# Opening of a fused gated cross-attention kernel: spare buffers for the second batch's turned tiles, another order of the first copies, identity products ahead of the first projections

## The reference, cut to what matters

```python
x = x + tanh(g_xattn[0]) * xattn(layernorm(x), ctx, pos, pos, Wq, Wkv, Wout, bout)
x = x + tanh(g_ffn[0]) * ffn(layernorm(x), up_w, down_w, expert_weight, ln_gamma, ln_beta)

# xattn: 16 batches, 256 rows, 512 columns, 32 heads of 16, context of 256 columns
q = rope(x @ Wq); k, v = split(ctx @ Wkv); k = rope(k)
attn = softmax(q @ k.T / 4) @ v
return attn @ Wout + bout
```

## Time and profile before

| what | us |
| --- | --- |
| median of the runs | 1657.44 |
| lowest and highest of the runs (3) | 1647.83 and 1659.67 |
| the profiled execution | 1645.12 |
| its span, from the first to the last instruction | 1643.3 |
| mean granted clock of TensorE in it | 0.982 |

### The profile page before, as it was taken

One profiled execution on the slowest core, in us unless ns is written; L12 is line 12 of the kernel. 1 busy time (PEld: TensorE's weight loads), 2 busy tenths in 40 slices (PEclk: granted clock), 3 DMA queues, 4 the chain that ended last, 5 costly groups with the idle time before them and its releaser, 6 DMA issues.

```text
span 1643.3 us, 27815 instructions
## 1 busy us (share of the span) xinstructions
PE 1558.6 (95%) x9760; PEld 1159.0 (71%) x9760; DVE 974.3 (59%) x1448; ACT 639.1 (39%) x962; POOL 295.5 (18%) x370
## 2 busy tenths in 40 slices
PE   6499999999999999988799999999999999999998
PEld 4356666666666666654578787887878878788786
DVE  6578887788777778865464543535435354263524
ACT  3155555555555555556342222222222222222221
POOL 5222222222222222201000210102101021020202
PEclk9699999999999999999899999999999999999999
DMA  4714444444444444333340110101101011010101
GB/s 141 158 47 112 121 108 117 123 123 116 116 104 103 106 102 116 96 94 99 115 135 20 45 33 10 48 20 46 32 1 53 25 46 32 1 51 26 36 16 39
DMA packets 67138, 120.53 MB, mean 73 GB/s; under 512 B 12280, under 2 KB 25720, under 8 KB 67064
## 3 DMA queue, kind: packets, MB, share of 16 engines
q1 hardware_dynamic: 67064, 119.50, 27.4%
HBM read 51.17 MB, written 16.78 MB: 41 GB/s over the span
## 4 chain that ended last, share of the span: by engine, by line
PE 82%; DVE 10%; issue 4%; ACT 1%; SPq 1%; POOL 1%; DMA 1%; DVEq 0%; POOLq 0%; ACTq 0%
PE pP L959 16%; PE pA L1142 11%; PE pO L959 11%; PE pB L1142 10%; PE pT L959 10%; PE pA L1044 6%; PE pO L1068 6%; PE pM L959 4%; DVE mneg L1339 3%; PE pB L1056 2%; PE pT L966 2%; PE pP L966 2%; PE pM L966 2%; PE pM L1109 1%; SPq L493 1%
## 5 line engine op out<-in xcount | busy, mean ns | idle before, releaser
L1339 DVE TENSOR_REDUCE mneg<-pA 128x4 f32<-128x1024 f32 x250 | 305.5, 1222 | 142.5 <-PE pA L1044 140.7
L864 ACT ACTIVATE probs<-pB 128x1024 f32<-128x1024 f32 x256 | 262.4, 1025 | 262.5 <-PE pB L1056 257.3
L1439 DVE TENSOR_TENSOR relu<-relu 128x512 f32<-128x512 f32 x128 | 88.2, 689 | 261.3 <-ACT hid L917 261.2
L687 POOL TENSOR_SCALAR var_eps<-meanvar 128x1 f32<-128x1 f32 x96 | 34.6, 360 | 1074.3 <-DVE meanvar L1231 1074.3
L1142 PE MATMUL pA<-dn,hid 128*128 128x512 f32 x768 | 199.0, 394 | 1.6 <-DVE hid L1441 0.9
L1142 PE MATMUL pB<-dn,hid 128*128 128x512 f32 x768 | 196.0, 390 | 0.0
L959 PE MATMUL pP<-fT,up 128*128 128x512 f32 x768 | 190.0, 396 | 0.0
L959 PE MATMUL pO<-fT,up 128*128 128x512 f32 x768 | 187.3, 393 | 0.0
L1142 PEld LDWEIGHTS pA<-dn,hid 128*128 128x128 f32 x768 | 142.9, 188 | 37.2 <-DVE hid L1441 5.9
L959 PEld LDWEIGHTS pO<-fT,up 128*128 128x128 f32 x768 | 144.5, 188 | 32.3 <-issue 0.4
L1142 PEld LDWEIGHTS pB<-dn,hid 128*128 128x128 f32 x768 | 144.2, 188 | 31.0
(11 more groups left out here) (177 smaller groups left out, 1958.1 us busy)
## 6 DMA issues: line engine op xcount, KB each, us to landing
stk<-kT SPq DMA_DIRECT2D x192, 128.0 KB, 2.9
stq<-qT SPq DMA_DIRECT2D x192, 128.0 KB, 3.0
xin<-x SPq DMA_DIRECT2D x32, 256.0 KB, 2.8
xres<-x SPq DMA_DIRECT2D x32, 256.0 KB, 3.0
x_scratch<-xres SPq DMA_DIRECT2D x32, 256.0 KB, 2.0
fx<-x_scratch SPq DMA_DIRECT2D x32, 256.0 KB, 2.7
fres<-x_scratch SPq DMA_DIRECT2D x32, 256.0 KB, 2.8
out<-y_s SPq DMA_DIRECT2D x32, 256.0 KB, 2.0
```

What stands on the lines that cost most here:

```text
L687: nc.gpsimd.tensor_scalar_add(var_eps[:], meanvar[:, 1:2], EPS).then_inc(ve_made, 1)
L864: nc.scalar.activation(probs[:, s % 4, :, :, :].rearrange("p a b s -> p a (b s)"), pB[:, :, :], ACT.Exp).then_inc(exp_done, 1)
L1339: nc.vector.tensor_reduce(mneg[par][:, :, 2 * u:2 * u + 2].rearrange("p t q -> p q t"), psum[:, :, :].rearrange("p q (t k) -> p q t k", t= ...
L1439: nc.vector.tensor_tensor(r[:], r[:], r[:], ALU.mult).then_inc(sq_made, 1)
```

## The change

- The turned tiles of batch 1 go to buffers that are idle in the opening: `k1T` (hi and lo) in parts 1 and 2 of `probs`, `q1T` in `av_s` (`turned_tiles`). So ACT no longer waits for the stack copies of batch 0 there. The copies of batch 1 count on semaphores of their own (`second_in`). ACT's first exponential, which writes `probs`, waits instead for all of batch 1's copies (`stack_in`).
- `rot2` has two buffers, taken in turn, and DVE's wait on POOL is one sum looser.
- SP issues the copies of the first half of the heads (k, then q) ahead of those of the second half, for both batches.
- ACT rounds all four query weight chunks ahead of the tables, and POOL splits chunks 2 and 3 ahead of `inv_std(2)`.
- `keep_awake` puts 22 products of the identity with itself ahead of X0 of batch 0, 28 ahead of K0 and 8 ahead of Q0, into a PSUM bank that the opening uses only later.

The diff:

```diff
--- before.py
+++ after.py
@@ -101,6 +101,7 @@
     ("X0", 1), ("qT0", 0), ("K0", 1), ("kT1", 0), ("qT1", 0), ("Q0", 1),
     ("X1", 1), ("kT0", 1), ("K1", 1), ("Q1", 1), ("kT1", 1), ("qT0", 1), ("qT1", 1),
 )
+AWAKE = {("X0", 0): 22, ("K0", 0): 28, ("Q0", 0): 8}
 FIRST = {0: ("V1",), 2: ("V0",), 11: ("m0",)}
 ORDER = {bank: [x for s in sorted(SCHEDULE) for x in SCHEDULE[s] if x[-1] != "<" and BANK[x] == bank]
          for bank in "PMT"}
@@ -227,7 +228,7 @@
         xnT = [sb1(f"xnT{i}", [P, KC, P], F32R) for i in range(2)]
         rot_q0 = sb1("rot_q0", [P, D])
         rot_k = sb1("rot_k", [P, D])
-        rot2 = sb1("rot2", [P, D])
+        rot2 = [sb1(f"rot2{i}", [P, D]) for i in range(2)]
         mT = [sb1(f"mT{i}", [NH // 2, S], F32R) for i in range(2)]
         rot_q1 = sb1("rot_q1", [P, D])
 
@@ -257,6 +258,15 @@
         def rot_of(name, b):
 
             return rot_k1 if opened(name, b) and name == "K1" else rot[name][:]
+
+        k1T = [probs[:, 1 + k, :, :, :].rearrange("p q t s -> p (q t) s").bitcast(F32R) for k in range(2)]
+        q1T = [av_s[:, KC * k:KC * (k + 1), :].bitcast(F32R) for k in range(2)]
+
+        def turned_tiles(x, b):
+
+            if opened(x + "T1", b) and b == 1:
+                return q1T if x == "q" else k1T
+            return [a[:] for a in (qT if x == "q" else kT)]
 
         pos_s = av_s[:, 0, 0:NT * POS].rearrange("p (n a) -> p n a", a=POS)
         ang = av_s[:, 1, 0:NT * ANG].rearrange("p (n a j) -> p n a j", a=POS, j=HALF)
@@ -331,6 +341,7 @@
         p_hi = sem("p_hi")
         roped = sem("roped")
         st_in = {x: [sem(f"st_in_{x}{h}") for h in range(2)] for x in "qk"}
+        second_in = {x: [sem(f"second_in_{x}{h}") for h in range(2)] for x in "qk"}
         a_done = sem("a_done")
         max_done = sem("max_done")
         m_done = sem("m_done")
@@ -395,6 +406,12 @@
         EARLY = CC + KC
         split_before = {"Q0": KC - 2, "V1": EARLY - 2, "O0": W1 - CC - 2}
 
+        def stack_in(x, half, b):
+
+            if opened(x + "T1", b) and b == 1:
+                return second_in[x][half], STACK_DMAS * INC
+            return st_in[x][half], STACK_DMAS * INC * (1 if isinstance(b, int) and b == 0 else b)
+
         def done_of(name, b):
 
             if opened(name, b):
@@ -484,7 +501,7 @@
                     sp.wait_ge(b_done, (b - 2) * STEPS + 8 * (half + 1))
                     alone(sp)
                 slots = slice(8 * half, 8 * half + 8)
-                dst, src, parts = (st_q[par], qT, Q_PARTS) if x == "q" else (st_k[par], kT, K_PARTS)
+                dst, parts, src = ((st_q[par], Q_PARTS) if x == "q" else (st_k[par], K_PARTS)) + (turned_tiles(x, b),)
                 sp.wait_ge(*taken_of(x + "T1", b))
                 alone(sp)
                 for r, part in enumerate(parts):
@@ -492,7 +509,7 @@
                         row, low = 64 * q + r, HALF_ROWS * half + PAIR * HD * q
                         sp.dma_start(dst[row:row + ROWS_A - r:len(parts), slots, :].rearrange("d (l c) s -> d l (c s)", c=KC).bitcast(F32),
                                      src[part][low:low + PAIR * HD, :, :].rearrange("p c s -> p (c s)").bitcast(F32)
-                                     ).then_inc(st_in[x][half], INC)
+                                     ).then_inc(stack_in(x, half, b)[0], INC)
 
             def load_max(b, par, half):
                 sp.wait_ge(taken[BANK[f"m{half}"]], number(f"m{half}", b))
@@ -579,7 +596,7 @@
                 sp.wait_ge(taken[BANK["qT1"]], number("qT1", B - 1))
                 for x in "qk":
                     for half in range(2):
-                        sp.wait_ge(st_in[x][half], STACK_DMAS * INC * B)
+                        sp.wait_ge(*stack_in(x, half, B - 1))
                 sp.wait_ge(taken[BANK["V0"]], number("V0", B - 1))
                 for t in range(TT):
                     sp.wait_ge(x1_out[t], INC * (BLK // S))
@@ -610,14 +627,14 @@
             load_raw(EARLY, W1)
             load_x(1, 1)
             sp.wait_ge(k_ones, 4 * INC)
-            for x in "kq":
-                for half in range(2):
+            for half in range(2):
+                for x in "kq":
                     load_stack(0, 0, half, x)
             load_x(2, 0)
             load_x(2, 1)
             load_ctx(2)
-            for x in "kq":
-                for half in range(2):
+            for half in range(2):
+                for x in "kq":
                     load_stack(1, 1, half, x)
             load_max(0, 0, 0)
             phase1(sp, iteration, ahead=1)
@@ -691,7 +708,7 @@
             def rope_sum(b, name):
                 pool.wait_ge(*taken_of(name, b))
                 t1 = rot_of(name, b)
-                nc.gpsimd.tensor_tensor(t1, t1, rot2[:], ALU.add).then_inc(roped, 1)
+                nc.gpsimd.tensor_tensor(t1, t1, rot2[ROPES.index(name) % 2][:], ALU.add).then_inc(roped, 1)
 
             def split_ctx(b, par):
                 pool.wait_ge(ctx_in, INC * (b + 1))
@@ -735,8 +752,8 @@
 
             inv_std(1)
             split_ctx(0, 0)
+            split_weights(CC + 2, EARLY)
             inv_std(2)
-            split_weights(CC + 2, EARLY)
             rope_sum(0, "K0")
             split_ctx(1, 1)
             rope_sum(0, "Q0")
@@ -822,14 +839,15 @@
                 elif name[0] == "a":
                     nc.scalar.copy(aT[0][:], turned_psum).then_inc(made, 1)
                 else:
-                    if some(b) and t == 0:
+                    if some(b) and t == 0 and not opened(name, b):
                         for half in range(2):
-                            act.wait_ge(st_in[name[0]][half], STACK_DMAS * INC * b)
+                            act.wait_ge(*stack_in(name[0], half, b - 1))
                             alone(act)
+                    hi = turned_tiles(name[0], b)[0]
                     if name[0] == "q":
-                        nc.scalar.mul(qT[0][:, :, cut], turned_psum, SCALE).then_inc(made, 1)
+                        nc.scalar.mul(hi[:, :, cut], turned_psum, SCALE).then_inc(made, 1)
                     else:
-                        nc.scalar.copy(kT[0][:, :, cut], turned_psum).then_inc(made, 1)
+                        nc.scalar.copy(hi[:, :, cut], turned_psum).then_inc(made, 1)
 
             def take_av(b, g):
                 act.wait_ge(av_done, GROUPS * b + g + 1)
@@ -858,6 +876,9 @@
                     if within(i):
                         if isinstance(i, int) and i == 0 and s == 0:
                             act.wait_ge(w_lo, W1 - CC - 2)
+                            for x in "kq":
+                                for half in range(2):
+                                    act.wait_ge(*stack_in(x, half, 1))
                         act.wait_ge(b_done, STEPS * i + s + 1)
                         if some(GROUPS * i + s // 2 - 1):
                             act.wait_ge(av_done, GROUPS * i + s // 2 - 1)
@@ -884,14 +905,13 @@
                 if name in TWO_STEP:
                     evacuate(name, b, b, opening_banks[n % len(opening_banks)], o_hi)
                 if n == 0:
-                    round_weights(CC, CC + 2)
+                    round_weights(CC, EARLY)
                     angle, turn = (a.rearrange("p n a j -> p n (a j)").unsqueeze(3).to_broadcast([P, NT, ANG, PAIR])
                                    for a in (ang, turns))
                     act.wait_ge(setup, 8)
                     for side, sign in enumerate((-1.0, 1.0)):
                         nc.scalar.activation(cos_t[:, :, side, :, :], turn, ACT.Sin)
                         nc.scalar.activation(sin_t[:, :, side, :, :], angle, ACT.Sin, scale=sign).then_inc(tables, 1)
-                    round_weights(CC + 2, EARLY)
                 if (name, b) == ("kT0", 0):
                     round_weights(EARLY, W1)
             later_setup()
@@ -981,9 +1001,15 @@
                 if half != 0:
                     last.then_inc(done[bank], 1)
 
+            def keep_awake(count):
+
+                for _ in range(count):
+                    nc.tensor.transpose(opening_banks[-1][:, 0:P], ident[:], ident[:])
+
             def opening():
                 banks = len(opening_banks)
                 for n, (name, b) in enumerate(OPENING):
+                    keep_awake(AWAKE.get((name, b), 0))
                     if (name, b) == ("K0", 0):
                         pe.wait_ge(wk_lo, CC)
                     if (name, b) == ("Q0", 0):
@@ -1032,7 +1058,7 @@
             def logits_a(b, par, s):
                 if s % 8 == 0:
                     for x in "kq":
-                        pe.wait_ge(st_in[x][s // 8], INC * STACK_DMAS * (b + 1))
+                        pe.wait_ge(*stack_in(x, s // 8, b))
                         alone(pe)
                 two = first_maxima(b, s)
                 if some(STEPS * b + s - (1 if two else 0)):
@@ -1254,9 +1280,9 @@
                     nc.vector.tensor_tensor(xnT[1][:], turned_psum, xnT[0][:].bitcast(F32),
```

(12 more changed lines are left out.)

## The result

The changed kernel has a median of 1662.73 us (1657.03 to 1672.32, 20 runs) beside 1644.95 us (1639.34 to 1659.67, 20 runs) for the kernel before. The ratio of the runs, with its 95% interval, is 1.0089 [1.0069, 1.0110], so it is 0.9% slower (the medians alone lie 1.1% apart). I had forecast 1644.1 us and a range of 1628 to 1654, so both are wrong. The profiled execution took 1659.59 us.

What follows compares the result with a forecast made beforehand. The opening's chain to the first logits was taken as the bound. Copies 5.7 + 0.8 = 6.5 us earlier, SP's 6.0 us wait gone and 0.8 us more made 13.3 us: 1657.44 - 13.3 = 1644.1 us, range 1628 to 1654.

Steps and rivals of the forecast that it cites:

- the first part: What bounds the kernel: the opening's chain up to the first logits for an exponential, at 81.55 us in the kernel before.
- The second batch's turned tiles: Opening: ACT's 10.8 us wait goes, gaining only SP's 6.0 us wait for turned maxima; the sum adds 0.8 us.
- Query weights sooner: Opening, batch 0: earlier query weight rounding and splits let Q0 start at 14.7 us, between 14.0 and 15.3.
- Identity products: Ahead of X0, K0 and Q0: warming raises TensorE's clock, so Q0 takes 3.0 instead of 5.38 us.
- From the rows of maxima to the logits: End of the opening: logits follow the issue of the maxima's rows by 4.96 us, with 0.8 us gained.
- The sum of the opening: Up to the first logits for an exponential: all gains of the change together, 13.3 us.
- the rival that it stays low longer after the early start: First batch's steps: TensorE's clock stays low, 60 us longer to be slower by 1%, about 1674 us; chance 0.03.
- The median: Base of the forecast: the gain was taken from 1657.44 us, since the profiled execution lay 12.3 us under it.

Runs made afterwards that it cites:

- e7: The kernel before with only the second batch's turned-tile buffers and their semaphores; 1645.56 us, ratio 0.9962.
- e1: The changed kernel without its 58 identity products; 1634.67 us, ratio 0.9922 to the kernel before.
- e3: The changed kernel with 30 identity products more, 14 ahead of qT1 of batch 1 and 16 behind the opening; 1635.12 us, ratio 0.9926 to the kernel before.
- e8: The changed kernel without second-batch buffers and identity products, keeping query weights sooner, new copy order and two rot2; 1642.74 us, ratio 0.9956 to the kernel before.
- e11: The changed kernel with PE's attention loop over the batches written out, other engines as they are; 1632.07 us, ratio 0.9924 to the kernel before.
- e12: The changed kernel with 22 identity products more, 10 ahead of qT1 of batch 1 and 12 behind the opening; 1634.46 us, ratio 0.9942 to the kernel before.
- e9: The kernel before, unchanged, profiled once more; median 1645.03 us, profiled execution 1657.0 us.
- e6: The kernel before with 40 semaphore increments in PE's stream ahead of X0 of batch 0; 1652.86 us, ratio 1.0010.
- e4: The kernel before with 116 semaphore increments in PE's stream ahead of X0 and K0 of batch 0, no products; 1677.57 us, ratio 1.0186.
- e10: The kernel before with 190 semaphore increments in PE's stream, placed where PE waits; 1645.84 us, ratio 0.9997.

## Why the prediction was wrong

**The step that failed** is the end of the first part: "all that the change does lies ahead of it, and behind it both kernels issue the same work in the same order". The order is the same, but PE's code lies 115 instructions further on. The 58 products were priced by their time in the opening alone (58 x 0.22 = 12.8 us of PE work at most), and the sum had no term for their place in the code. That term measured 30.3 us in five returns, 6.1 us each. No rival had it either. The prediction named the sign of it, "anything that differs past the first iteration would make the whole account wrong", without a mechanism or a chance.

**What could have told me.** The instruction queue's row stood in the page of before, 51 packets. Asked for the loop's stretch, the same view had none. PE executed 107 KB of code there again and again without a fetch, so the code had to be resident, and what is resident can be pushed out. And the phase 2 loop of the kernel before shows what the branch of a return with a fetch looks like:

```profile
L1178 PEldq COMPARE_BRANCH  x3: 83/3592/3870, 1113.7 to 1529.0; - x3
```

It costs PE nothing there: the branch at 1113.7 takes 3.87 us, and the matmuls of phase 2 follow each other without idle time from 1109.65 to past 1120. So the matmuls up to 1117.9 had been issued ahead of the branch. A long branch alone is thus no loss; what tells it is PE's idle time put down to "issue" behind it.

**The steps ahead of it**, by their numbers:

- *The second batch's turned tiles:* right. ACT's wait went, SP's wait of 6.0 us went, and the copies of batch 1 held nobody up: forecast 6.0 + 0.8, measured 7.25 us in the logits (e7).
- *Query weights sooner:* Q0 was taken to start at 14.7 between 14.0 and 15.3. It started at 15.59, 0.3 us beyond the upper bound. The rule of the Trainium skill's page SBUF — State Buffer (Who interferes with whom) agrees with the trace as to the contention: two VectorE splits took 2.38 us and GpSimd's two 3.16, where apart they took 1.28 and 2.67. The rest is ACT, which waited 2.00, 0.46 and 0.50 us for the query weights to land, where the prediction had "at once". In the five other profiles with this order (e1, e3, e8, e11, e12) ACT waited less and Q0 started between 14.66 and 15.10, within the bounds, though the splits held each other up there too (2.85 to 3.25 us on DVE, 2.97 to 3.03 on POOL). So what the bounds lacked was the wait for the weights.
- *Identity products:* as thought, they held up nothing: the 22 took 4.34 us and the 28 took 3.22, X0 started at 6.29 and K0 at 11.52, in 1.66 us. Q0 took 2.97 us (forecast 3.0). But their worth for the whole kernel isn't to be measured: e1 without them has the ratio 0.9922 and e3 with them 0.9926. The prediction gave them 2.4 us (5.38 - 3.0), of which 1.1 us are left at 68.92 against 69.98, and e8 had the high clock without them.
- *From the rows of maxima to the logits:* 68.92 - 64.87 = 4.05 us, the short end of the bounds (4.05 to 5.7), where the sum had 4.96 - 0.8. With 2.05 us to the start of the last issue, that leaves some 2.0 us for its landing, like the earlier trace rows, with 48 copies ahead of it in the queue. The 2.0 us of the Trainium skill's page DMA: Bandwidth & Descriptors (Anatomy of one DMA), which the prediction weighed, are given there for DMAs that GpSimd issues; these were issued by SP, and the landing agrees all the same.
- *The sum of the opening:* 13.3 forecast, 12.6 measured at the first logits and 13.2 at the first return. In kernels whose loop fits it carries through to the end: e1, e3, e11 and e12 are 0.6 to 0.8% under the kernel before, 9.5 to 12.8 us of 1645, where 13.3 were forecast.
- *The clock:* the rival that it stays low longer after the early start didn't come. Over 60 to 90 us the mean clock was 0.77 where it was 0.59 before.

**The median.** The forecast took its gain from the median of three runs, 1657.44 us, since the profiled execution was "12.3 us under the median". Over 20 runs the median is 12.5 us lower. An execution of that length, profiled in e9, had two stalled returns; the three first ones likely had some too, but of them no trace exists that shows it.

Four versions are well clear of both kernels: e11_unrolled 1632.07, e12_fit22 1634.46, e1_no_identity 1634.67 and e3_fit 1635.12 us. They can't be told from each other; e1 is the simplest, but its loop starts where that of the kernel before does, which stalled in e9. e11 has no return that could stall.

## What to carry to other kernels

Instructions put ahead of a loop also move it. Where a loop's body is of the size of several fetch blocks, look before any edit at the instruction queue's packets within its stretch, at the duration of its branch and at the engine's idle time behind it, and after the edit at all three again; a loop that fetches nothing is in a state that some harmless instructions can end. Instructions for warming are worth their place only if the same kernel without them is slower, and that is cheap to try. Where a few runs scatter by 1%, profile a long one before taking a median for the base. That other loops behave like this one no run here shows.

## What the runs showed of the hardware that I had not expected

- A loop body of 1,674 TensorE instructions, 107 KB, ran six times on one load. 115 more instructions ahead of it (a start after 1,932) cost 6.1 us at each return, and 159 to 189 more (1,976 to 2,006) nothing.
- A stalled return fetched nine packets of 256 instructions, more than the whole body, and the next return could be free again (e6, e9).
- The same kind of branch took 3.6 to 3.9 us in phase 2 and PE had no idle time there, since its matmuls were issued that far ahead.
- After 1,932 a return that fetches stops PE twice (the first return for 2.0 and 3.0 us with 0.7 us of work between), and the granted clock then falls (0.50 from 345 to 350 us). The other engines lose nothing of their own. That second loss is 2.2 us of the 6. In e9 each of the two stalled returns stopped PE once, for 3.0 and for 3.6 us.
- Near the lower edge the same kernel stalls in one execution and not in another: 0 and 2 of 5 returns in two profiles of the kernel before.
- An increment of a semaphore on PE took 0.15 us, so that 116 of them delayed the stack copies by 2.5 us (e4); 190 of them, put where PE waited, didn't delay the copies (e10: 36.09 against 36.44).
